# Attention in a transformer kernel: rope products grouped and moved behind the transposes, q steps ahead of scores, copies of q a slot earlier

## The reference, cut to what matters

```python
q_big = apply_rope(einsum(hidden_q @ Wq.T, w_kc_q))        # 192 features a head
q_r = einsum('bshq,hqr->bhsr', q_big, W_qr)
k_r = einsum('bld,hdr->bhlr', kv_r, W_kr)
attn = softmax(einsum('bhsr,bhlr->bhsl', q_r, k_r))
ctx_c = einsum('bhsl,bld->bhsd', attn, kv_r)
x = x + tanh(g) * (einsum(ctx_c, w_kc_kv) @ Wo.T)
```

## Time and profile before

| | before |
|---|---|
| median of 3 runs | 614.27 us (612.1 to 614.34) |
| the profiled execution | 611.38 us, span 609.2 us |
| PE busy | 529.5 us (87%) |
| DVE busy | 423.0 us (69%) |
| ACT busy | 289.9 us (48%) |
| POOL busy | 152.2 us (25%) |

### The profile page before, as it was taken

How to read it: one execution, slowest core, us unless ns; L and a number is a source line. 1 busy time by engine, 2 the same in 40 slices (tenths; PEclk the granted TensorE clock), 3 DMA queues, 4 the chain that set the end, 5 groups by cost and what they waited for, 6 DMA issues and landing times.

```text
span 609.2 us, 9266 instructions
## 1 busy us (share of the span) xinstructions
PE 529.5 (87%) x2762; PEld 381.6 (63%) x2762; DVE 423.0 (69%) x1122; ACT 289.9 (48%) x751; POOL 152.2 (25%) x150
## 2 busy tenths in 40 slices
PE   7787999987889998999999999999999866489980
PEld 3564687765578884566766666666666535368860
DVE  5898379996475547786868686868786886942324
ACT  3744543334545543363746455555545753135540
POOL 1032356652236532010100000000100003715660
PEclk9969989998799999999999999999999997779995
DMA  8669212221222219614141413212000900234416
GB/s 248 224 209 319 107 52 79 77 77 53 77 79 79 77 36 317 209 35 165 36 164 34 146 52 99 99 59 105 0 1 1 431 2 34 88 106 124 137 60 207
DMA packets 41872, 68.59 MB, mean 113 GB/s; under 512 B 4387, under 2 KB 31981, under 8 KB 41584
## 3 DMA queue, kind: packets, MB, share of 16 engines
q1 hardware_dynamic: 39584, 63.99, 32.3%
q0 software_dynamic: 2256, 4.20, 2.2%
HBM read 40.65 MB, written 29.49 MB: 115 GB/s over the span
## 4 chain that ended last, share of the span: by engine, by line
PE 61%; DVE 13%; issue 8%; POOL 6%; ACT 6%; DMA 3%; SPq 0%; DVEq 0%; POOLq 0%; ACTq 0%
PE bank L1342 10%; PE bank L1360 9%; PE bank L741 9%; PE bank L1393 5%; PE bank L1383 5%; PE bank L1404 4%; POOL y_rows L876 4%; PE bank L766 3%; DVE left L1727 3%; PE bank L1374 3%; DVE best L1722 2%; POOL xn_slots L870 2%; PE bank L1375 2%; PE bank L1241 2%; PE bank L1250 2%
## 5 line engine op out<-in xcount | busy, mean ns | idle before, releaser
L1547 ACT ACTIVATE silu<-bank,negm 128x256 f32<-128x256 f32 x128 | 59.5, 474 | 32.4 <-DVE negm L1774 32.2
L1555 ACT ACTIVATE probsT<-bank 128x512 f32<-128x512 f32 x64 | 38.3, 599 | 66.2 <-PE bank L1383 66.2
L1360 PE MATMUL bank<-qr,att_w_raw 128*64 128x512 f32 (+1 forms) x192 | 61.9, 605 | 1.6 <-issue 1.6
L1215 POOL TENSOR_TENSOR att_w_l<-att_w_raw,att_w_h 128x384 fp32r<-128x384 f32 x16 | 16.1, 1014 | 183.2 <-ACT att_w_h L1571 183.2
L663 POOL TENSOR_TENSOR ffn_w_l<-ffn_raw,ffn_w_h 128x512 fp32r<-128x512 f32 x30 | 38.9, 1297 | 66.5 <-ACT ffn_w_h L675 54.4
L687 ACT ACTIVATE hid_h<-hid 128x512 fp32r<-128x512 f32 x30 | 18.9, 631 | 69.8 <-DVE hid L702 47.7
L1774 DVE TENSOR_REDUCE negm<-bank 128x2 f32<-128x512 f32 x64 | 43.9, 686 | 5.9 <-PE bank L1375 4.9
L1782 DVE TENSOR_SCALAR hid<-silu,rden 128x256 f32<-128x256 f32 x128 | 45.2, 395 | 2.3
L1383 PEld LDWEIGHTS bank<-ident,hid 128*128 128x128 f32 x256 | 28.7, 140 | 26.8 <-issue 19.2
L1788 DVE SCALAR_TENSOR_TENSOR x<-bank,tg,x 128x512 f32<-128x512 f32 x32 | 23.8, 744 | 30.1 <-PE bank L1404 30.1
L1383 PE MATMUL bank<-ident,hid 128*128 128x128 f32 x256 | 40.0, 279 | 4.6 <-ACT probsT L1555 2.1
(11 more groups left out here) (225 smaller groups left out, 1275.2 us busy)
## 6 DMA issues: line engine op xcount, KB each, us to landing
xn_slots<-blank SPq DMA_DIRECT2D x8, 2048.0 KB, 8.4
ffn_raw<-in_w_ffn SPq DMA_DIRECT2D x30, 256.0 KB, 2.7
pair_w<-in_pair_w SPq DMA_DIRECT2D x8, 768.0 KB, 5.9
moe_w<-in_w_moe SPq DMA_DIRECT2D x1, 6144.0 KB, 17.8
folds<-att_w_raw SPq DMA_DIRECT2D x6, 896.0 KB, 8.2
att_w_raw<-folds SPq DMA_DIRECT2D x12, 384.0 KB, 3.3
moe_x<-xn_slots SPq DMA_DIRECT2D x31, 128.0 KB
ffn_raw<-in_w_ffn SPq DMA_DIRECT2D x30, 128.0 KB, 2.3
```

The source lines that it names most:

```text
L1360: last = nc.tensor.matmul(bank[2][cols, :], g_of(w_raw[b], 2 * j + w)[:, cols], qr[n % JT][:, w, :], start=(first and w == 0), stop=(not f ...
L1547: last = nc.scalar.activation(ex[u % 2][:, h, :], bank[4 + u % 2][:, h * S:(h + 1) * S], ACT.Exp, bias=negm[:, u % 2, h:h + 1], accum_out= ...
```

## The change: what it does

- Rope: all six products of a half are issued in one call, in slots 3 (half 0) and 9 (half 1), where before the half-width ones stood in slots 2 and 8 and the full-width ones in 3 and 9. The order of the six is the same. Their semaphore now counts three at the end of a group.
- PE's order in a slot: q step, scores, transposes, projection, rope, values, where before it was scores, rope, transposes, q step, values, projection. Values that fall in the slot behind a rope group (slots 4 and 10) are moved to that slot's beginning.
- q step 2 goes from slot 1 to slot 2, on PE and with its multiplications on DVE.
- The copy of q of half 0, with the low part, goes from slot 6 to slot 5. Half 1 stays in slot 10.
- DVE's wait ahead of a q step's multiplications is for the whole rope group before, instead of for the one product that reads the same buffer.

```diff
--- before.py
+++ after.py
@@ -1061,11 +1061,11 @@
         def g_of(w, j):
             return w[:, GOFF + j * P:GOFF + (j + 1) * P]
 
-        Q_AT = {0: 1, 1: 2, 4: 3, 5: 4, 7: 5}
+        Q_AT = {0: 1, 2: 2, 4: 3, 5: 4, 7: 5}
         J_OF = (0, 2, 1)
         EARLY = 11
-        R_AT = {2: (0, 1), 3: (2,), 8: (3, 4), 9: (5,)}
-        QH_AT = {6: 0, 10: 1}
+        R_AT = {3: 0, 9: 1}
+        QH_AT = {5: 0, 10: 1}
 
         Q3_AT = {m: n for n, m in Q_AT.items()}[JT]
 
@@ -1345,22 +1345,22 @@
                             m += 1
                     last.then_inc(s_q, 1)
 
-                def rope_step(i, b, loads, ns):
-
-                    c, first = ns[0] // JT, ns[0] % JT == 0
-                    if first:
+                def rope_step(i, b, loads, c):
+
+                    if c == 0:
                         pe.wait_ge(s_g[b], loads * 16)
-                    if first and not (isinstance(i, int) and i + c == 0):
+                    if not (isinstance(i, int) and i + c == 0):
                         pe.wait_ge(s_ql, i * 2 + c)
-                    for w in range(2):
-                        pe.wait_ge(s_cs, i * 12 + (2 * ns[-1] + w + 1))
-                        for n in ns:
-                            j = J_OF[n % JT]
-                            cols = (slice(0, C), slice(0, P), slice(C, P))[j]
-                            last = nc.tensor.matmul(bank[2][cols, :], g_of(w_raw[b], 2 * j + w)[:, cols],
-                                                    qr[n % JT][:, w, :], start=(first and w == 0),
-                                                    stop=(not first and w == 1), skip_group_check=True)
-                    last.then_inc(s_rp, len(ns))
+                    for ms in ((0, 1), (2,)):
+                        for w in range(2):
+                            pe.wait_ge(s_cs, i * 12 + (2 * (c * JT + ms[-1]) + w + 1))
+                            for m in ms:
+                                j = J_OF[m]
+                                cols = (slice(0, C), slice(0, P), slice(C, P))[j]
+                                last = nc.tensor.matmul(bank[2][cols, :], g_of(w_raw[b], 2 * j + w)[:, cols],
+                                                        qr[m][:, w, :], start=(m < 2 and w == 0),
+                                                        stop=(m == 2 and w == 1), skip_group_check=True)
+                    last.then_inc(s_rp, JT)
 
                 def scores(j, jb, u):
                     if u % 4 == 0:
@@ -1407,20 +1407,22 @@
 
                 def slot(n, i, b, loads, do_s, do_q):
                     j, jb = i - 1, 1 - b
+                    if do_s and n in VALUES_AT and n - 1 in R_AT:
+                        values(j, VALUES_AT[n])
                     if early(n, i, do_q):
                         q_step(i + 1, 1 - b, 0)
+                    if q_here(n, i, do_q):
+                        q_step(i, b, Q_AT[n])
                     if do_s and n < NU:
                         scores(j, jb, n)
+                    if do_s and LAG <= n < NU + LAG:
+                        transpose_probs(j, n - LAG)
+                    if do_s and n in PROJECT_AT:
+                        project(j, jb, PROJECT_AT[n])
                     if do_q and n in R_AT:
                         rope_step(i, b, loads, R_AT[n])
-                    if do_s and LAG <= n < NU + LAG:
-                        transpose_probs(j, n - LAG)
-                    if q_here(n, i, do_q):
-                        q_step(i, b, Q_AT[n])
-                    if do_s and n in VALUES_AT:
+                    if do_s and n in VALUES_AT and n - 1 not in R_AT:
                         values(j, VALUES_AT[n])
-                    if do_s and n in PROJECT_AT:
-                        project(j, jb, PROJECT_AT[n])
 
 
                 def first_q_step():
@@ -1753,7 +1755,7 @@
                     cos_sin(0, 0, 6)
                 def cos_sin(i, n, bk=None):
                     if n >= JT or not (isinstance(i, int) and i == 0):
-                        dve.wait_ge(s_rp, i * (2 * JT) + (n - JT + 1))
+                        dve.wait_ge(s_rp, i * (2 * JT) + (n // JT) * JT)
                     dve.wait_ge(s_q, i * 6 + (n + 1))
                     q2 = bank[n % 2 if bk is None else bk][:].rearrange("p (b s) -> p b s", b=2)
                     for w, tab in ((0, cosq), (1, sinq)):
```

## The result

The kernel after takes 653.89 us (median of 4 runs, 650.38 to 657.99) against 613.76 before: a ratio of 1.0666, interval 1.0621 to 1.0712. It is slower, as forecast, but by 40 us instead of 28, and outside the range of 626 to 649.

What follows compares the result with a forecast made beforehand. PE's issue was taken to bound the loop, DVE next at 77%. Seven pairs at +3.9 us, plus 0.7 in pair 0 and 0.3 in the last, made 28.3 us: 642 us forecast, range 626 to 649.

Steps and rivals of the forecast that it cites:

- What bounds, and the mechanism: Seven-pair loop: bound by PE's issue; lost softmax cover and q's copy open waits, +3.9 us a pair; chance 0.81.
- The joints: PE's switches between kinds of products in a pair: count stays the same, costing +0.1 us a pair.
- POOL's pieces keep their slots: 0: Outside the seven pairs: POOL's pieces stay in their slots, so they add 0.
- upper end, at 4.7 us a pair: Forecast mechanism's top: DVE's steps 0.04 us longer each, or a POOL piece falling on a scaling.
- Full clock taken for granted: Loop: pair profiled at full clock, its durations used for the layout; no cost for a slower clock entered.
- Pair 0: Rope now behind PE's 2.18 us wait: q step 3 2.0 us later, stage end 0.7 later, bounds 0 and 2.1.
- Last pass: Last pair: values 0 ahead of scores 4 and transposes 2, mostly in a stretch awaiting DVE; 0.3 us, bounds 0 and 1.1.
- Front only: Rival: only transposes 0 and 1 lose, the middle hides; 1.3 us a pair, 624 us; chance 0.12.
- the middle hole: PE ahead of transposes 5: q's copy and low part hold normalise 5 back, a wait of 1.62 us.
- The group without joints: Rival: the rope and values group runs without joints, present waits go; -1.1 us a pair, 606 to 607; chance 0.04.
- No effect: Rival: DVE and ACT run ahead of the layout, leaving +0.1 us a pair and 1.0 outside; 616 us; chance 0.03.

Runs made afterwards that it cites:

- run 11: Kernel after with the second weight piece in slot 9 instead of 6, behind all scalings of the pair: 644.8 us, ratio 1.051.
- run 4: Kernel before with only the copy of q of half 0 in slot 5 instead of 6: 623.31 us, ratio 1.0148.
- run 5: Kernel before with only the rope products grouped in slots 3 and 9, ahead of the transposes, with DVE's coarser wait: 618.94 us, ratio 1.0143.
- run 6: Kernel before with only PE's q steps put ahead of the scores of their slot: 611.43 us, ratio 0.9981.
- run 3: Kernel after with rope ahead of the transposes again and values 0 and 3 at the end of their slots: 638.72 us, ratio 1.0389.
- run 7: Kernel after with values at the end of their slots in the last pass alone: 651.69 us, ratio 1.0644.
- run 9: Kernel after with the second weight piece in slot 8 instead of 6: 649.96 us, ratio 1.0611.
- run 8: Kernel after with six more products, which nobody reads, between scores 7 and transposes 5: 652.47 us, ratio 1.064.
- run 10: Kernel after with six unread products between scores 7 and transposes 5 and the second weight piece in slot 8: 650.8 us, ratio 1.0641.
- run 12: Kernel after with the second weight piece in slot 9 and six unread products between scores 7 and transposes 5: 642.57 us, ratio 1.046.
- run 13: Kernel before with only PE's q steps ahead of the transposes of their slot: 608.92 us, ratio 0.9925.

## Why the prediction was right and where it was wrong

**What bounds, and the mechanism: right.** The cover that rope had given to transposes 0 and 1 went, and the copy of q in slot 5 pushed normalise 5 back. The starts that the text worked out for transposes 0, 1, 5 and projection 1 came within 0.03 us, and with the two disturbances taken out the pair lasted 36.00 us (run 11) against the forecast's 32.17 + 3.9 = 36.1. Three parts of the change were also made alone in the kernel before: the copy's slot cost 1.6 us a pair (run 4), the group 0.6 (run 5), q ahead of scores nothing (run 6). That is 2.2 of the 3.8 us. Rope behind the transposes was only undone in the kernel after, together with the place of values: 34.96 (run 3) against 36.00 makes it 1.0. The rest, about 0.6, and the slot of q step 2 were not tested alone.

**The joints: right.** A rope group and the start of values are 3.78 us apart (318.40 to 322.18) against 1.87 + 1.82 + 0.10. The new joints cost what their kin in the earlier trace rows cost, and the count stayed at twelve. The Trainium skill's statement in "TensorEngine Tiling (Array Packing)", Key Properties, that a change of mode drains the engine, agrees with run 5, where grouping alone saved nothing.

**"POOL's pieces keep their slots: 0": wrong.** The slots are kept, but what else runs in that time isn't. ACT's exponentials 6 and the weight split behind them came late together, and POOL's piece began 0.12 us behind the start of the scalings of tile 6. They ended 0.15 us behind it (313.63 and 313.48), after 1.36 instead of 0.62 us. Transposes 7 started 26.75 us behind the first scores at full clock (run 7) and 26.0 with the piece out of the way (run 11). I had the collision only as an upper end, at 4.7 us a pair. With it the pair lasts 36.75 at full clock. The Trainium skill, "SBUF — State Buffer", Terms, says that DVE and GpSimd have one pair of ports in common, that it is locked for a whole instruction, and that the loser waits; this trace agrees, with 1.36 and 1.09 us in the rows above, and with runs 9 and 11, where the cost followed the piece and then went. A collision by itself isn't the loss, and one could be seen before the change. In the pair of the earlier trace rows POOL's first piece holds the scalings of tile 2 just so, and PE waits for nothing there:

```profile
323.69 1.41 DVE L1782 TENSOR_SCALAR hid<-silu,rden 128x256 f32<-128x256 f32 x2
```

```profile
323.95 1.01 POOL L1215 TENSOR_TENSOR att_w_l<-att_w_raw,att_w_h 128x384 fp32r<-128x384 f32 x1 [19.22 <-ACT att_w_h L1571]
```

In runs 3 and 4 the scalings of tile 6 take 1.36 and 1.39 us and cost nothing either, since rope products still stand ahead of the transposes behind them. The change brought POOL's second piece onto these scalings and took away the cover behind them.

**Full clock taken for granted: wrong.** I costed every product at 2.4 GHz since the loop before had PEclk 1.00. In the kernel after six stretches of 3.4 us at 1.2 GHz lie in the loop, each beginning within 0.8 us behind the start of projection 1. Their net cost is 0.67 us a pair (run 7), less than the 1.6 us they add to the products (34.53 against 32.96 busy), since at full clock transposes 7 would have waited 0.91 us for the held scalings anyway. The two costs lie beside each other, not one behind the other.

The loop's ladder in numbers: 224.9 us before, 250.5 by the order alone (run 11), 254.9 with POOL's collision (runs 8 and 9), 258.9 with the clock. The forecast had 27.3 for the first step (the seventh pair, without an early q step behind it, grew by 2.5 us only, which I hadn't taken apart) and nothing for the other two. Each number is that of one profiled execution. Between the profiled executions before and after lie 42.3 us, 14.0 more than forecast: 6.7 in the loop, 3.7 in pair 0, 3.2 in the last pass, 3.2 behind it, less the 2.9 ahead of pair 0.

**Pair 0, 0.7 forecast within 0 to 2.1: wrong.** It took 24.5 instead of 20.1 us. In the kernel after:

```profile
232.60 1.97 PE L331 MATMUL bank<-ident,xn 128*128 128x128 f32 x8 [4.05 <-DVE xn L316]
234.50 5.46 PE L1360 MATMUL bank<-qr,att_w_raw 128*64 128x512 f32 x12
```

With the rope pair gone from the hole, PE idles 4.05 us at a stretch instead of 2.18, and the clock is at half for 6.8 us from 230.9 on, within this gap. The transposes and the rope group take 6.8 us (232.60 to 239.39), where 1.25 and 3.6 would do at full clock: 1.9 us for the clock. Q step 3 starts 12.4 us behind q step 2 instead of 8.7, and the stage takes 12.1 from there instead of 11.4. So 2.5 of the 4.4 us would be left at full clock, by this estimate: the 1.8 by which the rope pair puts q step 3 back, all of it, and 0.7 behind it. I had let DVE's queue take up all but 0.7. The profiles of all eleven kernels with no rope products in slot 2 have a half clock stretch there, and none of the four that keep them. The Trainium skill, "TensorE: Matmul & The Clock Gate", under HAM oscillation, describes how the clock falls after a gap between bursts of products; the rows here agree, with 4.05 us of gap and the half clock behind it. The stretches in the loop had no such gap ahead of them (1.5 us at most). I had the 2.18 us wait and the 1.87 us of rope in hand, and didn't add them to one gap.

**Last pass, 0.3 within 0 to 1.1: wrong.** Values ahead of scores cost 1.2 us (run 7), which is the whole of the block that I had called mostly covered: nothing covers it, the softmax chain is bare there. The half clock adds 2.4 here; three kernels with the same last pass had none in it (24.15).

**Behind it, nothing forecast.** The last 111 to 115 us contain 37 to 49 us at half clock in every kernel, 11 us more of them after than before. They vary by 3 us between kernels that don't differ there, so I can't call them part of the change.

**The rivals.** Front only fell: the middle hole came with 1.48 us. The group without joints fell with run 5. No effect fell.

**Open.** What decides whether a stretch at half clock falls into a pair. It fell in the kernel after (six of seven pairs), in run 7 (five), and in three pairs of run 3, and in none of runs 9 and 11 with the same 1.5 us hole, nor in run 4 with 1.65. The order of work alone doesn't decide it, since pairs of the same code have it and don't. Nor is it tied to one product: in the kernel after the stretches start 37.55 us apart, the pairs 37.42, so each begins later behind projection 1 than the one before (0.1 to 0.75 us). Run 8, with the hole filled, had none where its twin, the kernel after, had six. But the twins of runs 10 and 12, runs 9 and 11, had none without filling either, and each is one profiled execution, so the filling isn't shown to be a cure. That there are several idle places within a few us of each other may be the ground; no run shows it.

## What to carry to other kernels

Where engines work through lists in fixed order, lay the lists beside each other with the trace's own durations for one full period: that gave 36.1 us a pair where 36.00 came, and it found the better order too (run 13: put independent work ahead of the step that waits, not behind it). Then do two checks that such a layout doesn't make by itself: which operations of DVE now coincide with one of POOL and have nothing on PE to cover them, and where a gap of PE grows by the work that is taken out of it, with half the clock perhaps behind it. An operation that seems to fill a hole for free may be what keeps the clock up (in pair 0 all eleven kernels without it had the half clock, and none of the four with it).

## What the runs showed of the hardware that I had not expected

- PE's clock fell to half in a loop in which PE was 92% busy and its longest gap 1.5 us (34.55 of 37.42 us above).
- The price of the same 3.4 us stretch at half clock depends on what lies beside it: 1.49 us a pair in run 3 (36.45 against 34.96), 0.67 in the kernel after, where the slowed products ran while delayed scalings were awaited.
- Adding 1.4 us of unread products to each pair (run 8 against the kernel after) didn't make the kernel slower: 652.47 against 653.89 us.
